# Second attention: queries and keys projected transposed and spread to the heads' rows by DMAs, instead of transposed by TensorE

## The reference

```python
qkv = (x @ Wqkv + bqkv).reshape(b, s, 3, H, hd)        # H = 16 heads, hd = 16
q, k, v = (qkv[:, :, 0], qkv[:, :, 1], qkv[:, :, 2])
def rot(t):
    t1, t2 = jnp.split(t, 2, axis=-1)                  # first and second 8 features of a head
    return jnp.concatenate([t1 * c - t2 * si, t1 * si + t2 * c], axis=-1)
q, k = rot(q), rot(k)
scores = einsum('bthd,bshd->bhts', q, k * scale)       # causal, softmax, times v, out projection
```

## Time and profile before

| | |
|---|---|
| device time of three runs | 668.51 median, 667.05 lowest, 672.08 highest |
| the profiled execution: device time, span | 670.2, 668.2 |
| granted clock of TensorE, mean over the span | 0.983 |
| PE busy | 646.3 us, 97% of the span |
| PEld (weight loads) busy | 557.3 us, 83% |
| DVE, ACT, POOL busy | 512.6 (77%), 493.6 (74%), 389.6 (58%) |
| chain of waits that ended last | PE 80%, DVE 7%, POOL 4%, ACT 3%, issue 3% |

### The profile page before, as it was taken

One profiled execution on the slowest core, in us unless ns is written; L12 is line 12 of the kernel. 1 busy time (PEld: TensorE's weight loads), 2 busy tenths in 40 slices (PEclk: granted clock), 3 DMA queues, 4 the chain that ended last, 5 costly groups with the idle time before them and its releaser, 6 DMA issues.

```text
span 668.2 us, 15602 instructions
## 1 busy us (share of the span) xinstructions
PE 646.3 (97%) x5214; PEld 557.3 (83%) x5214; DVE 512.6 (77%) x1868; ACT 493.6 (74%) x1305; POOL 389.6 (58%) x644
## 2 busy tenths in 40 slices
PE   8989999999999999999999799999999999999996
PEld 5668988999898899899978688889787787778985
DVE  2977999967988898667988655466689989848554
ACT  3988887978688886799897566674846687876652
POOL 3468657574676755788869445555782331536651
PEclk9999999999999999999999799999978999999999
DMA  9651022223122120410031030112020000010310
GB/s 336 181 148 55 22 64 50 87 50 103 42 63 80 46 86 23 111 34 2 1 120 48 0 93 3 48 49 79 17 88 10 4 4 4 3 48 1 122 52 33
DMA packets 27445, 40.29 MB, mean 60 GB/s; under 512 B 4059, under 2 KB 19939, under 8 KB 27365
## 3 DMA queue, kind: packets, MB, share of 16 engines
q1 hardware_dynamic: 27076, 38.84, 19.1%
q10 hardware_dynamic: 288, 0.46, 0.3%
HBM read 29.19 MB, written 1.05 MB: 45 GB/s over the span
## 4 chain that ended last, share of the span: by engine, by line
PE 80%; DVE 7%; POOL 4%; ACT 3%; issue 3%; SPq 2%; DMA 1%; DVEq 0%; POOLq 0%; ACTq 0%
PE bank L1386 69%; PE bank L1400 8%; PE bank L1692 2%; SPq L2904 1%; DVE bank L2543 1%; POOL probs L2653 1%; DMA qT<-xT_plain 1%; POOL w_split_lo L2653 1%; ACT x L1836 1%; DVE bn L2195 1%; POOL qT L2653 1%; DMA qT<-rope_buf 1%; DVE bilinear L2175 0%; ACT probs L2078 0%; POOL stat L2653 0%
## 5 line engine op out<-in xcount | busy, mean ns | idle before, releaser
L2650 POOL TENSOR_SCALAR probs<-probs,soft 128x256 f32<-128x256 f32 (+1 forms) x256 | 104.3, 429 | 52.4 <-DVE soft L2331 51.2
L1940 ACT ACTIVATE probs<-probs,soft 128x256 f32<-128x256 f32 (+1 forms) x256 | 113.0, 445 | 11.8 <-DVE soft L2323 11.3
L1386 PE MATMUL bank<-xT_hi,w_split_hi 128*128 128x512 f32 x256 | 103.6, 405 | 1.5 <-DVE xT_lo L2172 1.0
L2653 POOL TENSOR_TENSOR w_split_lo<-w_raw,w_split_hi 128x512 fp32r<-128x512 f32 (+2 forms) x57 | 74.9, 1323 | 47.0 <-ACT w_split_hi L1829 46.9
L1386 PE MATMUL bank<-xT_lo,w_split_hi 128*128 128x512 f32 x256 | 100.4, 392 | 0.0
L1386 PE MATMUL bank<-xT_hi,w_split_lo 128*128 128x512 f32 x192 | 75.5, 393 | 0.0
L2323 DVE CUSTOM_DVE_ANT_0 probs<-bank,front_pack 128x128 f32<-128x128 f32 (+1 forms) x192 | 57.5, 331 | 20.1 <-PE bank L1386 19.0
L1829 ACT ACTIVATE probsT<-bank 128x384 f32<-128x384 f32 x128 | 54.1, 495 | 16.2 <-PE bank L1400 15.8
L2653 POOL TENSOR_TENSOR probs<-probs 128x512 f32<-128x512 f32 x32 | 44.6, 1407 | 32.2 <-ACT probs L2021 31.6
L1386 PE MATMUL bank<-keyT,qT 128*64 128x64 f32 (+3 forms) x768 | 60.1, 301 | 0.7 <-POOL qT L2653 0.7
L1386 PEld LDWEIGHTS bank<-xT_hi,w_split_hi 128*128 128x128 f32 x256 | 48.2, 188 | 14.7 <-issue 3.2
(11 more groups left out here) (261 smaller groups left out, 1905.5 us busy)
## 6 DMA issues: line engine op xcount, KB each, us to landing
w_raw<-in_w_front SPq DMA_DIRECT2D x8, 768.0 KB, 4.5
w_raw_heads<-in_w_back SPq DMA_DIRECT2D x8, 640.0 KB, 4.5
qT<-xT_plain SPq DMA_DIRECT2D x56, 64.0 KB, 2.0
qT<-rope_buf SPq DMA_DIRECT2D x40, 64.0 KB, 2.0
qT_first<-xT_plain SPq DMA_DIRECT2D x32, 64.0 KB, 2.0
w_raw<-in_w_gateT SPq DMA_DIRECT2D x8, 256.0 KB, 2.6
w_raw<-in_w_upT SPq DMA_DIRECT2D x8, 256.0 KB, 3.4
w_raw<-in_w_downT SPq DMA_DIRECT2D x8, 256.0 KB, 3.7
```

What stands on the lines that cost most here:

```text
L1386: return t.matmul(out, lhsT, rhs, start=start, stop=stop, skip_group_check=shared)
L1940: ins = s.activation(p[:, at], p[:, at], ACT.Exp, bias=st[:, 0, r:r + 1], scale=-1.0, accum_out=st[:, 1, r:r + 1])
L2650: return g_.tensor_scalar(out, in0, s1, s2, op0, op1)
L2653: return g_.tensor_tensor(out, in0, in1, op)
```

## The change

Queries and keys come out of the projection already transposed. For each batch, i now means query (0) or key (1) instead of the token tile. The weights are stationary (their columns reordered on the host by `spread_order`), x's transpose moves: 12 matmuls of 128x256 and no bias matmul. A row of the result is feature r (of 8) of one half, for 16 heads at once. DVE adds the bias per row and multiplies by cos and sin in four 128x256 instructions; POOL adds and subtracts (two of 128x256). ACT makes one high copy into a new ring split1, POOL one low part in place. A new step **spread b i** on SP then copies rows to where the heads need them: six DMAs of 128 KB each (four of the high part, two of the low), [128 partitions x 256] to [16 partitions x 8 x 256]. Query rows of batches 2 and 3 also get one DMA that zeroes the maxima's rows. The constant rows are DMAs too (step **late**, 4 of 128 KB for each of the two places). The qkT step is gone with its transposes and copies; the rings q1 and k1 have two places, each of which holds a whole batch. top_T writes its rows with one DMA instead of four. The feed-forward's late buffers use the memory of qT1 and kT1 instead of q_rows and k_rows.

```diff
-N_PROBS, N_QT, N_QK1 = 8, 4, 5
+N_PROBS, N_QT, N_QK1 = 8, 4, 2
+NHALVES1, HALF1 = 2, HD1 // 2
+PARTS1 = (("hi", "hi", "lo"), ("lo", "hi", "hi"))
...
             elif name == "qkv":                                  # PE
-                mm(out, ones1[:, :], bias1[:, 0:2 * D], True, False)
-                for c in range(DC):
-                    ins = mm3(out, xT_pair[:, c, at], w_qkv[:, c, 0:2 * D], False, c == DC - 1)
+                for half in range(NHALVES1):
+                    first = i * D + half * P
+                    ins = mm3_chunks(out[:, half * S:(half + 1) * S], [(w_qkv[:, c, first:first + P], xT_pair[:, c, cols(b)])
+                                                                       for c in range(DC)], half == 0, True)
...
-            elif name == "qkT":                                  # PE; its ACT and DVE copies go too
-                        for t_ in range(GH // 2):
-                            ins = t.transpose(out[...], rows_of_head(rows)[:, i, first:first + P], ident1)
...
             elif name == "qkv":                                  # DVE
-                tt(r0, qk, rope1[:, i, 0, :].unsqueeze(1).to_broadcast([P, 2 * H1, HD1]), ALU.mult)
-                tt(r1[:, :, 0:hd], qk[:, :, hd:HD1], sin[0], ALU.mult)
-                tt(r1[:, :, hd:HD1], qk[:, :, 0:hd], sin[1], ALU.mult).then_inc(qk_turned.sem, 1)
+                for half in range(NHALVES1):
+                    bias = qk_bias[:, NHALVES1 * i + half:NHALVES1 * i + half + 1]
+                    stt(cos_part[:, half, :], qk[:, half, :], bias, rope1[:, 0, :], ALU.add, ALU.mult)
+                    ins = stt(sin_part[:, 1 - half, :], qk[:, half, :], bias, rope1[:, 1, :], ALU.add, ALU.mult)
...
             elif name == "qk_split":                             # ACT
+                w.wait_ge(*latest(e_down_ready, [(E_ROUTED, h, TH // 2 - 1) for h in range(NHALF)]))
+                copy(split1[split1_turns.place[b, i]][:, :], probs[in_probs.place["qk", b, i]][:, :]).then_inc(qk_hi.sem, 1)
...
+    def qk1_free(b, i):
+        before = (q1_turns, k1_turns)[i].before[b,]
+        if before is None:
+            return [last_expert()] if b else []
+        return [latest(st1_ready, [(before[0], h) for h in range(H1)])]
...
+            elif name == "spread":                               # SP
+                for left in qk1_free(b, i):
+                    w.wait_ge(*left)
+                if i == 0 and b >= N_QK1:
+                    q.dma_start(rows_of_top(...), zeros...)
+                for part, left in (("hi", qk_hi), ("lo", qk_lo)):
+                    w.wait_ge(*left[b, i])
+                    for at in [at for at, wanted in enumerate(PARTS1[i]) if wanted == part]:
+                        for half in range(NHALVES1):
+                            q.dma_start(rows_of_kind((qT1, kT1)[i][place], NHALVES1 * at + half), src[:, half, :])
```

More of the change, by code:

```diff
@@ L685, in make_plan @@
     every_expert = [("e_down", e, h) for e in range(NE) for h in range(NHALF)]
-    stage(("rows1",), "POOL 4", *[("att_mix", b) for b in range(B)], *[("e_u", 0, h) for h in range(NHALF)])
+    for n in range(N_QK1):
+        stage(("late", n), "SP 2.0, DMA 2.0, WAY 2", *every_expert if n else [],
+              *[("att_mix", b) for b in range(B)], *[("e_u", 0, h) for h in range(NHALF)])
+    stage(("rows1",), "POOL 1.5", *[("att_mix", b) for b in range(B)], *[("e_u", 0, h) for h in range(NHALF)])
     for b in range(B):
@@ L689, in make_plan @@
         for i in range(TB):
-            stage(("qkv", b, i), "PE 1.68, DVE 1.28, POOL 1.28", ("xT", "attn1", b), ("split", U_QKV, 0), ("consts",),
+            stage(("qkv", b, i), "PE 1.52, DVE 1.92, POOL 1.5", ("xT", "attn1", b), ("split", U_QKV, 0), ("load", "attn1"),
                   holds=[bank("qk", b, i, left=(("qkv", b, i), "DVE")), Hold("rope1", (b, i), By(("qkv", b, i), "POOL")),
-                         Hold("probs", ("qk", b, i), By(("qk_split", b, i), "POOL"))])
-            stage(("qk_split", b, i), "ACT 1.06, POOL 1.4", ("qkv", b, i), ("rows1",),
-                  *[By(("qkT", b - 1, g), "PE") for g in range(G1) if b], items=2)
+                         Hold("probs", ("qk", b, i), By(("spread", b, i), plan.LAST))])
+            stage(("qk_split", b, i), "ACT 0.57, POOL 1.37", ("qkv", b, i), *[("e_down", E_ROUTED, h) for h in range(NHALF)],
+                  holds=[Hold("split1", (b, i), By(("spread", b, i), plan.LAST))])
+            stage(("spread", b, i), "SP 2.8, DMA 1.0, WAY 2", ("qk_split", b, i), *every_expert if b else [],
+                  holds=[Hold("qk"[i] + "1", (b,), By(("st1", b, G1 - 1, GH // 2 - 1), "PE"), (b % N_QK1,))])
         stage(("v1", b), "PE 1.48, ACT 0.6", ("xT", "attn1", b), ("split", U_QKV, 0), ("consts",), ("rows1",),
@@ L2809, in pool_program @@
[L2809 to L2814 removed]
+                t = probs[in_probs.place["qk", b, i]]
```

522 lines of the change are left out of this document (256 added, 266 removed), and 65 rows, old and new, of the table ASIDE.

## The result

The changed kernel takes 667.6 us (median of 20 executions, 661.8 to 673.8) where the kernel before takes 671.3 beside it: ratio 0.9938, 95% interval 0.9912 to 0.9965. That is 0.6% faster, within the 1% that was called no change. Over all executions the two means are 670.4 and 667.7, 0.4% apart. The forecast was 6.7 us less, the profiled executions differ by 668.2 - 664.0 = 4.2 us of span, and the medians by 3.6.

The account below looks back on a forecast made before the run. TensorE, busy in 97% of the span, was taken as the bound, with DVE close behind in the attention. +5.7 - 11.5 + 1.5 - 2.4 = -6.7 us gave 663.5 on the profiled scale, 661.8 against the median; range 652 to 674.

Parts of the forecast that it names:

- The order elsewhere and the router: Router's place, 371 to 379 us: -2.4 us; everywhere else the lists' order costed at 0, give or take 2.
- 1.6 earlier, and 0.8 of a shorter half-clock time: Router's place: u_pair_lo comes 1.6 us earlier and half clock behind PE's wait shortens by 0.8, together -2.4 us.
- the lists hold the same work: Everywhere outside the costed places, same work with PE at its limit: 0, give or take 2 us.
- The start: Ahead of the first scores: PE waits some 3.7 us for g_pair_lo, half clock follows, first mask starts later: +5.7 us.
- The steady part: Attention from first mask to 577.6 us: DVE becomes the larger load, 83.1 us shrink to 71.6: -11.5 us.
- 66.6 / 0.93: Attention from first mask to 577.6 us: DVE's remaining 66.6 us of work at 93% busy give 71.6 us.
- 4.4 us before the scores: Batch 0's spread: twelve issues at 0.63 us, the last landing 4.4 us before the scores want it, so hidden.
- The hand-overs: Buffers passing between batches, twice: up to 10.7 us of SP's queue and landing, mostly covered by DVE's work: +1.5 us.
- The prediction's signs: First mask to last out1: DVE above 90%, PE about 90%, clock 0.95 or more.
- the rival that the clock takes the slack: Attention: PE's small idle pieces lower the clock, -11.5 shrinks to -3.8 or nothing: 667 to 675 us, chance 0.21.
- The rule cited beside it: Beside the clock's rival: small idle times between groups of matmuls can be enough to let the clock swing between levels.
- The bare hand-over: Buffers passing between batches without DVE's cover, each costing up to 10.7 us plus 3 at half clock: 682; chance 0.12, over 675.

Follow-up runs that it names:

- a1: The kernel before, old attention kept, with the changed kernel's order, priorities and costs of the steps ahead of it: 665.6 us, ratio 0.994 to the kernel before.
- a4: The changed kernel with DVE's e_split 6 1 moved ahead of e_down 7 1's four sums: 667.7 us, ratio 0.997 to the kernel before.
- a2: The changed kernel with the DMA of the maxima issued by ACT on its own queue instead of SP's: 667.1 us, ratio 0.997 to the kernel before.
- b1: The changed kernel with the old order of everything ahead of the attention: 688.5 us, ratio 1.027 to the kernel before.
- c1: b1 with three pairs on SP's queue turned back to the changed kernel's order: 680.2 us, ratio 1.010 to the kernel before (1.019 by all executions).
- a3: The changed kernel with two feed-forward loads moved on SP's queue behind batch 0's fourth maxima: 664.4 us, ratio 0.993 to the kernel before.

## Why the prediction came out as it did

The two profiled executions can be laid beside each other, stage by stage. Up to the end of e_split 7 1's two g_pair_lo: -8.9 us, where the forecast had -2.4. From there to the first mask: +5.3, for +5.7. From it to the last batch's out1: -2.2, for -11.5 + 1.5 = -10.0. Behind that: +1.6, for 0. Together -4.2, for -6.7. So the sum came as near as it did by luck: 7.8 us that the attention did not give were mostly made up by 6.5 that the order ahead of it gave unforeseen.

- **The order elsewhere and the router: named too small.** Forecast -2.4 and "0, give or take 2". Idle and half-clock time on PE up to 476 us fell from 15.2 to 8.9. What failed here is "1.6 earlier, and 0.8 of a shorter half-clock time": the gap did not shrink, it closed, and took all 5.3 us at half clock with it; and a wait of 1.86 us at 47 us, with 3 us at half clock behind it, also went. a1 has nothing but this part of the change, and its gain is as large as the change's. I had costed "the lists hold the same work" at nothing, in a change that rewrote them all. Of before, timeline of PE:

```profile
47.68 0.55 PE L1400 MATMUL bank<-identity,probs 128*128 128x128 f32 x3 [1.86 <-POOL probs L2650]
```

- **The start: right.** The wait ahead of e_down 6 1 is 2.98 us (3.7 forecast) and half clock follows it, as said. From the end of e_split 7 1's two g_pair_lo, where the forecast counts from, to the first mask it is 494.48 - (477.62 + 2.61) = 14.25 us before and 490.85 - (470.04 + 1.28) = 19.5 now: +5.3 for +5.7. The four new DVE instructions start 0.39 to 0.40 apart, 1.6 us in all (1.65 forecast):

```profile
470.04 1.28 DVE L2183 TENSOR_TENSOR g_pair_lo<-probs,g_pair_hi 128x512 fp32r<-128x512 f32 x2
...
487.65 0.48 DVE L2186 SCALAR_TENSOR_TENSOR probs<-bank,attn_pack 128x256 f32<-128x256 f32 x1
488.05 0.48 DVE L2186 SCALAR_TENSOR_TENSOR rope_tmp<-bank,attn_pack 128x256 f32<-128x256 f32 x1
...
490.85 0.30 DVE L2546 CUSTOM_DVE_ANT_0 bank<-bank,tri 128x128 f32<-128x128 f32 x1
...
584.51 0.69 DVE L2183 TENSOR_TENSOR y<-bank,x 128x512 f32<-128x512 f32 x1 [0.53 <-PE bank L1417]
```

  Of before, the two rows that these differences need beside the earlier trace rows (timeline of DVE):

```profile
477.62 2.61 DVE L2172 TENSOR_TENSOR g_pair_lo<-probs,g_pair_hi 128x512 fp32r<-128x512 f32 x2
...
590.35 0.69 DVE L2172 TENSOR_TENSOR y<-bank,x 128x512 f32<-128x512 f32 x1 [0.65 <-PE bank L1386]
```

- **The steady part: the step that failed.** "66.6 / 0.93" took the whole stretch as undisturbed, with no wait for a DMA in it and no half clock. Where it is undisturbed, DVE reaches 90 to 96% and PE 96 to 100%, so the 0.93 was fair. But from the first mask to the last batch's out1 (12.7 us further than the 577.6 up to which the forecast counted) it took 584.51 - 490.85 = 93.7 us, against 590.35 - 494.48 = 95.9 before: -2.2 where -11.5 + 1.5 was forecast. The two stretches, before and now:

```profile
494.48:590.35 95.87, 93.63 (x976) 75.49 (x975) 83.47 (x391) 72.98 (x190) 34.22 (x70) 0.96 0.08 24
490.85:584.51 93.66, 84.53 (x857) 66.80 (x854) 77.73 (x379) 62.16 (x168) 31.64 (x66) 0.91 0.32 81
```

  PE's work, counted at full clock, fell by 12.7 us (89.6 to 76.9). Its idle time rose by 6.9 (2.2 to 9.1), what it lost to half clock while busy by 3.7 (4.0 to 7.7). The prediction's signs say the same: PE at 90% as forecast, but DVE at 83% instead of above 90%, and a clock of 0.91 instead of 0.95. So DVE did not become the limit over the stretch. Most of the loss stands in 490 to 536 us, with 6.4 us idle and 7.7 at half clock. Waits for DMAs are only a part of it: 1.39 and 1.88 us of the idle time, and the low from 528.5. The larger low, from 497.5 on, came behind small waits for DVE and ACT, at a time when DVE was busy throughout (7.50 of 7.50 us from 490 to 497.5), so at the start of the attention DVE was the limit, and PE's small waits for it came with half clock.
- **The spread's first batch.** The issue price was right (0.63), "4.4 us before the scores" was not. Landing took a median of 3.1 us on the page, where I took 2.0 from 64 KB DMAs; the cover was about 1 us, and a4 spent it.
- **The maxima behind batch 1's spreads: overlooked.** I followed SP's queue at the hand-overs only. At the start of the attention it has the same fault, top_T 0 0 behind two loads and one spread, top_T 0 1 behind the next.
- **The hand-overs.** 9.2 us of SP for the 8.2 worked out, waits of 1.88 and 0.67 for 2 x 0.8. What was missing is the 7 us at half clock behind the first: +5 to 6 and not +1.5 (an estimate: the two waits and half of 7). That the wait is the cause of that half clock is argued and not shown: a2 took the wait away, and in its profiled execution the clock was at half from 497.5 to 531.5.
- **The rivals.** The forecast was wrong in size and the range held the time, by the luck named above. What came true is the rival that the clock takes the slack. At the start of the attention it came by the rival's own road, small waits of PE for DVE and ACT ahead of the low from 497.5; at the hand-over by another, a wait of 1.88 us for a DMA; and a thin stretch stands behind both. The rule cited beside it, of the Trainium skill, page "TensorE: Matmul & The Clock Gate", section "A second HAM failure mode: psum-queue depth-cycling", is not borne out where nothing else disturbs: 554 to 578 has 0.84 us of small idle time at clock 1.00. Ahead of 497.5 the small waits come to 2.8 us in 6, and there the trace agrees with it in kind. The bare hand-over did not come, neither in the change nor in b1, whose wait of 4.00 us is for the first spread of batch 0.

What stays open: why c1's clock loss is 10 us above that of the change, whose attention is almost the same, why filling helps the one and not the other, and how much of the change's own clock loss is due to its waits for DMAs and how much to its small waits for DVE and ACT, which no run took away. The steady part's missing 7.8 us are measured; their cause is shown only in part, since the edits that took single waits away (a2, a3, a4) lowered the time by 3.3 us at most.
